# Eight matmuls between two small transposes in a fused state-space and quantised feed-forward kernel

## The reference

```python
u = einsum('bld,nd->bln', layernorm(x), W_in)        # N = 64 states
h = h * Abar + u_t * Bbar                            # scan along the tokens
x = x + einsum('bln,dn->bld', h * C, W_out)
xn = layernorm(x)
def quant_act(x):                                    # per token
    scale = 127.0 / clip(max(abs(x), axis=-1), EPS)
    return clip(round(x * scale), -128, 127) / scale
hid = gelu(quant_act(xn) @ ternary(w1).T)            # 1024 -> 4096
x = x + quant_act(hid) @ ternary(w2).T               # 4096 -> 1024
```

## Time and profile before

| | us |
|---|---|
| median of 3 runs | 2173.85 (2166.89 to 2175.21) |
| the profiled execution | 2172.28 |
| its span, slowest core (core 5) | 2170.7 |
| spans of the other seven cores | 2149.3 to 2163.6 |
| busy on core 5: VectorE | 1447.5 (67%) |
| TensorE, matmul | 1248.3 (58%) |
| ScalarE | 444.2 (20%) |
| GpSimd | 218.6 (10%) |

### The profile page before, as it was taken

The page is one execution under the profiler, slowest core; times in us unless marked ns, Lnnn a source line. Parts: engine busy times, 40 slices in busy tenths (PEclk is TensorE's granted clock), DMA queues, the critical chain, the costliest instruction groups (busy, mean ns, idle before and its releaser), DMA issues.

```text
span 2170.7 us, 33812 instructions; the slowest of 8 cores (2149.3 to 2170.7 us)
## 1 busy us (share of the span) xinstructions
PE 1248.3 (58%) x12248; PEld 871.4 (40%) x12248; DVE 1447.5 (67%) x2155; ACT 444.2 (20%) x682; POOL 218.6 (10%) x164
## 2 busy tenths in 40 slices
PE   0002222211221147887788778877887788778887
PEld 0002112111111145654565456545654565456553
DVE  3665555565566566777777777767777777777753
ACT  0002222211111022221222223222221223222210
POOL 0000000122112100100010001000100011001000
PEclk9999999999999988898899899988898899989998
DMA  5973444111111100100000001000100000001000
GB/s 145 319 242 127 135 145 137 57 39 58 59 50 47 39 1 21 40 11 30 11 36 34 11 30 40 11 30 11 40 30 11 30 31 21 30 11 40 11 20 21
DMA packets 30825, 120.15 MB, mean 55 GB/s; under 512 B 3972, under 2 KB 3972, under 8 KB 28612
## 3 DMA queue, kind: packets, MB, share of 16 engines
q1 hardware_dynamic: 15428, 56.63, 8.0%
q0 software_dynamic: 9712, 38.28, 5.0%
q10 hardware_dynamic: 5520, 23.07, 3.2%
HBM read 101.19 MB, written 16.78 MB: 54 GB/s over the span
## 4 chain that ended last, share of the span: by engine, by line
DVE 47%; PE 21%; DMA 13%; issue 8%; ACT 5%; DVEq 3%; POOLq 2%; ACTq 1%; SPq 0%; POOL 0%
DVE hred L634 10%; PE pm1b L771 8%; DMA vs<-w 8%; DVE vs L657 7%; PE pm1a L771 6%; DVE k L658 5%; DMA xbT<-xh 4%; DVE xn L591 2%; PE pout L828 2%; DVE TLblk L574 2%; DVE TLblk L607 2%; POOLq L252 2%; ACT L344 2%; DVE x L507 2%; DVE x L505 2%
## 5 line engine op out<-in xcount | busy, mean ns | idle before, releaser
L828 PE MATMUL pout<-t2T,k 128*128 128x512 bf16 x2048 | 512.6, 414 | 4.9 <-DVEq L539 4.9
L828 PEld LDWEIGHTS pout<-t2T,k 128*128 128x128 bf16 x2048 | 211.3, 105 | 284.1 <-issue 91.7
L771 PE MATMUL pm1b<-k1fm,t1T 128*128 128x128 bf16 x4096 | 264.1, 225 | 0.0
L771 PE MATMUL pm1a<-k1fm,t1T 128*128 128x128 bf16 x4096 | 259.1, 223 | 2.8 <-ACTq L339 2.8
L771 PEld LDWEIGHTS pm1b<-k1fm,t1T 128*128 128x128 bf16 x4096 | 247.5, 101 | 0.0
L771 PEld LDWEIGHTS pm1a<-k1fm,t1T 128*128 128x128 bf16 x4096 | 242.6, 100 | 6.5 <-issue 3.4
L634 DVE TENSOR_REDUCE hred<-h_sb 128x128 f32<-128x4096 f32 x32 | 226.4, 7076 | 27.2 <-ACTq L339 21.5
L657 DVE TENSOR_TENSOR vs<-h_sb,sc2bc 128x1024 f32<-128x1024 f32 x128 | 156.9, 1226 | 89.5 <-ACTq L368 75.6
L791 PE MATMUL pT<-identb,xn 128*128 128x128 bf16 x512 | 53.5, 268 | 244.4 <-DVEq L593 244.4
L732 PE MATMUL pT<-identb,k 128*128 128x128 bf16 x512 | 64.7, 306 | 189.4 <-DVEq L511 189.4
L250 POOL TENSOR_TENSOR xn<-xbT 128x1024 f32<-128x1024 f32 x64 | 121.0, 1890 | 367.5 <-DMA xbT<-xh 219.8
(11 more groups left out here) (153 smaller groups left out, 1274.9 us busy)
## 6 DMA issues: line engine op xcount, KB each, us to landing
xbT<-xh SPq DMA_DIRECT2D x16, 1024.0 KB, 5.0
xbT<-xo SPq DMA_DIRECT2D x16, 1024.0 KB, 5.3
out<-out_s POOLq DMA_DIRECT2D x32, 512.0 KB, 3.0
h_sb<-w SPq DMA_DIRECT2D x11, 1024.0 KB, 7.2
vs<-w ACTq DMA_DIRECT2D x11, 1024.0 KB, 7.3
vs<-w ACTq DMA_DIRECT2D x22, 512.0 KB, 3.6
h_sb<-w SPq DMA_DIRECT2D x21, 512.0 KB, 3.5
k<-w POOLq DMA_DIRECT2D x10, 1024.0 KB, 7.1
```

The lines of the kernel that those rows point to most:

```text
L771: ti = t.matmul(reg, t1T[:, k * 4096 + m * 128:k * 4096 + (m + 1) * 128], k1fm[oi % 2][:, k * 128:(k + 1) * 128], start=(k == 0), stop=(k ...
L828: ti = t.matmul(pout[:, d * 512:(d + 1) * 512], k2[:, hk * 128:(hk + 1) * 128], t2T[:, hk * 1024 + d * 512:hk * 1024 + d * 512 + 512], sta ...
```

## The change

`te_btr` gets a switch `pre` and is called twice. The first call does L810 alone. The second does the transpose of `sc2` and the spreading product. Between the two calls stand tiles 24 to 27 of the second product, that is 8 of the 16 matmuls that used to follow; the other 8 follow as before. No semaphore, buffer or transfer is changed, and the other engines' programs are the same.

```diff
-            def te_btr(oi, b):
-                t.wait_ge(S["hmax"], oi + 1)
-                t.wait_ge(S["uev"], min(b + 2, NIT))
-                t.transpose(pmisc[:, 128:256], hred[:],
-                            ident32[:]).then_inc(S["hmaxT"], 1)
+            def te_btr(oi, b, pre=True):
+                if pre:
+                    t.wait_ge(S["hmax"], oi + 1)
+                    t.wait_ge(S["uev"], min(b + 2, NIT))
+                    t.transpose(pmisc[:, 128:256], hred[:],
+                                ident32[:]).then_inc(S["hmaxT"], 1)
+                    return
                 t.wait_ge(S["sc2_"], oi + 1)
                 t.transpose(pmisc[0:1, 256:384], TL["sc2"][:, 0:1],
                             ident32[:]).then_inc(S["rowT"], 1)
...
                 if has1:
-                    te_btr(oi1, b)
+                    te_btr(oi1, b, pre=True)
                 if has2:
-                    te_mm2(oi2, range(24, 32))
+                    te_mm2(oi2, range(24, 28))
+                if has1:
+                    te_btr(oi1, b, pre=False)
+                if has2:
+                    te_mm2(oi2, range(28, 32))
```

## The result

The changed kernel takes 2261.91 us (median of 10 runs, 2252.21 to 2270.73) against 2171.79 us: ratio 1.042, 95% interval 1.0396 to 1.0443. The forecast was 2252 us, range 2210 to 2278. In the profiled execution the spans are 2243.1 to 2254.1 us (2149.3 to 2170.7 before), and the mean granted clock is 0.904 to 0.909 on the eight cores (0.930 on core 5 before). The slowest core is now core 1; its rows are shown.

What follows compares the result with a forecast made beforehand. TensorE's delays at L813 and from L753 to L598 were taken to bound each round. 2172.3 us + 45 (late L813) + 34 (colder restart) = 2251, with the other cores 2252 us; range 2210 to 2278 us.

Steps and rivals of the forecast that it cites:

- What bounds: The 43.48 us loop between L634s: TensorE delays at L813, or in the first product from L753, lengthen the round.
- Term 1: Between L810 and L813: the eight moved matmuls run mostly at half clock and delay L813; 45 us in sum.
- 24 of 28 rounds at half from L810 on: Clock count at L810 in the old profile; each such round was to delay L813 by 1.7 us.
- Term 2: From L753 to L598: longer idle time before L753 makes the first product restart at half clock; 34 us in sum.
- the 18 us that I subtracted: At L753 to L598: cold restarts already paid by the kernel before, 11 rounds at 1.63 us.
- little more to lose: Other cores, with rounds nearly all of the short kind, lose slightly more, raising the forecast from 2251 to 2252 us.
- The sum: Whole kernel: profiled time plus both terms, with a little for the other cores, gives 2252 us.
- Delay only: Rival: late L813 as forecast, but the restart at L753 costs nothing more; 2217 us, chance 0.18.
- Cold throughout: Rival: from L810 through L753 the clock stays low and every restart is the longest kind; 2283 us, chance 0.12.
- TensorE takes what is ready first: Rival: at L813 the eight matmuls fill only free time, so no change; 2172 us, chance 0.03.
- The gap keeps the clock up: Rival: with matmuls in the gap the clock never falls around L810 and restarts are warm; 2145 us, chance 0.04.
- what would show it: Profile signs: L815 3.4 to 3.8 us behind L811, idle before L753 above 2.5 us, L753 to L598 at least 14.

Runs made afterwards that it cites:

- eight before L810: Changed kernel with tiles 24 to 27 (8 matmuls) moved ahead of the first small transpose, nothing between the transposes; 2212.94 us, ratio 1.0172 to the kernel before.
- fill before L753: Changed kernel plus 7 extra matmuls with unused results in the idle time before the scan's product; 2212.54 us, ratio 1.0162 to the kernel before.
- both idle times were filled: Changed kernel plus unused matmuls, 14 before the first small transpose and 18 before the scan's product, in full rounds only; 2158.69 us.
- both filled in the old order: Kernel before plus unused matmuls in full rounds, 14 before the first small transpose and 11 before the scan's product; 2205.16 us.
- sixteen in the gap: Changed kernel with all 16 matmuls of tiles 24 to 31 between the two small transposes, none behind the spreading product; 2308.98 us.
- four in the gap: Changed kernel with only tiles 24 and 25 (4 matmuls) between the small transposes, 12 matmuls behind the spreading product; 2182.95 us.
- old order with the fill before L810 only: Kernel before plus 14 unused matmuls before the first small transpose, in the 28 full rounds; 2167.48 us.

## Why the prediction was right, and where not

**What bounds.** Right. Every us at L813 and every us between L753 and L598 came out of the round unchanged: the three stretches that the terms do not touch kept their length to 0.01 us.

**Term 1** was forecast at 45 us and is 31.6 - 5.1 = 26.5 (27.8 by the mean of the eight cores). The mechanism is right (0.24 + 8 x 0.427 us in the cold rounds, L815 right behind). What failed is the step "24 of 28 rounds at half from L810 on", each at 1.7 us. The count was read too high: in the kernel before L810 took 0.45 us, its length at half clock, in 20 of the 28 rounds and 0.30 to 0.42 in the other eight. And the old clock history was carried over to the new kernel. After the change 22 of 27 rounds did start at half, but only 13 stayed there through all eight; in 9 the clock rose near their end and L815 was 1.2 us late instead of 1.6. In these 9 and in the 5 that were at full clock, L815 to L657 is mostly 1.79 us and not 2.25. I had given that saving to a rival only. Whether the moved matmuls themselves or the changed length of the round raised the clock in the 9 was not tried.

**Term 2** was forecast at 34 us and is 42.9 in the 27 rounds of the slowest core, 53.4 by the mean of the eight cores, with most of the 8.6 us of the end beside it, where I had put nothing. Two steps were sized too small. The first is the price of a cold restart: 14.82 us against the warm 12.53 is 2.3 us, and I had taken 1.85, from the 16 matmuls behind L816. The 16 matmuls were the wrong model: in 13 rounds the 32 matmuls of the group behind L753 took 3.62 us and the next group up to 2.5, after L753, L755 and L741 had run at half clock as well. Which of these short steps keeps the clock down was not tried. The second is what the kernel before paid already: the 18 us that I subtracted were core 5's, whose 11 slow rounds are the most of any core, and the "little more to lose" on the others, for which I had put 1 us, was 6 in the mean of the spans (89.6 against 83.4). That the restart is cold in every round held.

**The sum** was right to 10 us (2262 against 2252) partly by luck, because errors cancel: by the mean of the eight cores term 1 is 28 and not 45, term 2 is 53 and not 34, and the end adds 8.

**Rivals.** *Delay only* is excluded by the runs with eight before L810 and with fill before L753. *Cold throughout* had the restart at 2.9 us where 2.3 were measured and 1.85 forecast, and was wrong for the gap. *TensorE takes what is ready first* is excluded by every cold round: L815 waits for all eight. *The gap keeps the clock up* was right as a mechanism and wrong for this kernel: it works when L810 is reached at full clock, as the runs with fill show, and the 3.58 us of idleness ahead of L810 prevent that in most rounds (22 of 27; with the fill in front of it, in none). Its price of -27 us meant rounds of 42.5 us, and 42.34 were measured once both idle times were filled.

Of what would show it: L815 at 3.4 to 3.8 us held in 13 of 27 rounds, an idle time above 2.5 us and L753 to L598 above 14 us in all 27, and the lowest rounds are 44.06 us, none of 42.6.

## What to carry to other kernels

Ready work put in front of a waiting step is free only if it fits at the clock that TensorE has there, not at its best. VectorE's answer comes about 1.9 to 2.0 us behind the first transpose: eight at full clock fitted (L815 at 1.88 us), eight at half did not (3.65), four at half did (2.03). Ask also where the work was taken from: here it had kept TensorE busy up to a second step of the critical path, and its absence cost more than its presence in front of the first (53 us against 28 in the full rounds). Which idle time to fill first the runs do not say: in the changed kernel either fill alone gave about 1.7 us a round, and both 3.7. In the changed order, full rounds of 42.38 us with both idle times filled, against 46.06 with none, agree with the advice of the Trainium skill ("TensorE: Matmul & The Clock Gate", section "Why this matters for your kernels") against idle gaps between bursts. It is not enough by itself: with both filled in the old order the clock still fell, and the rounds took 44.23 us, more than the 43.05 of the kernel before.

## What the runs showed of the hardware

- The length of the idle time does not tell what the restart costs once it is above 3 us. L753 to L598 took 15.3 us after 3.3 us of idleness and 14.4 after 5.1 in the changed kernel, but 14.4 after 5.4 and 15.2 after 6.8 with sixteen in the gap (means of such rounds; 12.53 when warm). What sorts them was not found out. With four in the gap the idle time was 2.1 us in the mean, and it took 12.53 us in half of the rounds.
- In the slow rounds of the kernel before L753 itself still ran at full clock (0.37 us after 2.02 us of idleness) and the clock fell behind it. In the changed kernel L753 found half clock in all 27 rounds, after 3.05 to 5.42 us.
- In the old order with both fills the first small transpose found full clock, three small steps with waits between them followed, 2.5 us in all, and the clock fell to half 1.5 to 2.4 us behind that transpose in every full round. With eight matmuls among the same steps it stayed at 1.00. The small steps alone do not settle it: in the old order with the fill before L810 only the fall came 1.5 to 4.2 us behind the transpose, and in one round not at all before the 16 matmuls were through.
- 32 extra matmuls in every full round, whose results nobody uses, made the changed order 0.7% faster than the kernel before; 25 in the old order made it 1.5% slower.
